# Scan over image rings: four strided history entries a ring, turned to rows one by one

## The reference

```python
# layer 0: relu, 3x3 depthwise convolution with dilation 2, 1x1 convolution, folded batch norm; x is (32, 56, 56, 256)
# layer 1: a scan over the pixels of the 56x56 image in spiral order, from the centre outwards
def step(g, inp):
    ci, ni, nm, nc = inp                       # this pixel, its four neighbours, their mask, their count
    local = g[:, ci, :]
    neigh = (g[:, ni, :] * nm[None, :, None]).sum(axis=1) / nc
    u = jnp.concatenate([local, neigh], axis=-1)
    y_sc = jnp.tanh(u @ w1 + b1) @ w2 + b2     # w1 is (512, 512), one scalar per image
    return g.at[:, ci, :].set(local + y_sc[:, None] * w_y[None, :]), None
```

## Time and profile before

| | |
|---|---|
| three runs, median | 4940.8 us (4936.70 to 4956.19) |
| the profiled execution, its span | 4956.47 us, 4954.6 us |
| busy share of the span | PE 91%, PEld 66%, DVE 81%, ACT 51%, POOL 70% |
| chain that ended last, by engine | PE 70%, ACT 10%, DVE 9%, issue 7%, DMA 2% |
| waits in the scan | PEld L868 for DVE L768: 197.5 us, 256 times; DVE L768 for ACT L554: 194.3 us, 344 times; PE L859 for DVE L704: 155.3 us, 293 times |

### The profile page before, as it was taken

One profiled execution on the slowest core, in us unless ns is written; L12 is line 12 of the kernel. 1 busy time (PEld: TensorE's weight loads), 2 busy tenths in 40 slices (PEclk: granted clock), 3 DMA queues, 4 the chain that ended last, 5 costly groups with the idle time before them and its releaser, 6 DMA issues.

```text
span 4954.6 us, 62164 instructions
## 1 busy us (share of the span) xinstructions
PE 4515.9 (91%) x19323; PEld 3290.4 (66%) x19323; DVE 4011.1 (81%) x6107; ACT 2520.8 (51%) x4454; POOL 3487.0 (70%) x2478
## 2 busy tenths in 40 slices
PE   3999999999999999999999999888888888888875
PEld 2788888888788888888878887644444444444432
DVE  5888888988886888888888887288888888877753
ACT  3566666666566566656656665333444443333321
POOL 3888888888887888888888888566666655554321
PEclk7999999999999999999999999999999999999976
DMA  3344444444444444444444443499999988876530
GB/s 92 116 130 139 132 138 134 135 137 134 132 137 135 132 139 131 138 129 140 131 137 132 139 127 126 168 310 298 294 317 288 285 273 259 242 226 188 166 107 27
DMA packets 395139, 835.31 MB, mean 169 GB/s; under 512 B 76864, under 2 KB 178496, under 8 KB 394688
## 3 DMA queue, kind: packets, MB, share of 16 engines
q1 hardware_dynamic: 251408, 420.08, 31.3%
q0 software_dynamic: 143408, 411.26, 22.2%
HBM read 419.95 MB, written 425.85 MB: 171 GB/s over the span
## 4 chain that ended last, share of the span: by engine, by line
PE 70%; ACT 10%; DVE 9%; issue 7%; DMA 2%; POOL 1%; SPq 0%; DVEq 0%; POOLq 0%; ACTq 0%
PE psum L846 12%; PE psum L848 12%; PE psum L847 12%; PE psum L830 12%; PE psum L859 10%; DVE psum L704 4%; ACT relu_rows L531 4%; PE psum L819 3%; PE psum L868 3%; PE psum L878 2%; PE psum L880 2%; DMA out<-dw_rows 2%; ACT u_hi L554 2%; PE psum L879 2%; ACT psum L549 2%
## 5 line engine op out<-in xcount | busy, mean ns | idle before, releaser
L629 DVE SCALAR_TENSOR_TENSOR dw_rows<-relu_rows,taps,dw_rows 128x1792 f32<-128x1792 f32 x872 | 1805.2, 2081 | 25.4 <-ACT dw_rows L520 20.3
L445 POOL DMA_INDIRECT s_x<-xo,wave_idx x784 | 1365.5, 1742 | 315.3 <-issue 215.9
L464 POOL DMA_INDIRECT out<-dw_rows x897 | 891.9, 994 | 860.4 <-DVE dw_rows L712 623.8
L846 PE MATMUL psum<-w_hi,u_hi 128*128 128x512 f32 x3136 | 1385.1, 442 | 0.0
L451 POOL DMA_INDIRECT s_pre<-eo,wave_idx x784 | 1207.8, 1541 | 247.5 <-issue 229.5
L848 PE MATMUL psum<-w_hi,u_lo 128*128 128x512 f32 x3136 | 1233.3, 393 | 0.0
L847 PE MATMUL psum<-w_lo,u_hi 128*128 128x512 f32 x3136 | 1226.4, 391 | 0.0
L859 PE MATMUL psum<-dw_rows,ident 128*128 128x512 f32 x1794 | 978.7, 628 | 161.5 <-DVE near L704 155.3
L485 ACT ACTIVATE eo<-psum 128x512 f32<-128x512 f32 x784 | 468.1, 597 | 1222.9 <-PE psum L848 1123.9
L549 ACT ACTIVATE psum<-psum 128x512 f32<-128x512 f32 x897 | 522.1, 582 | 914.2 <-PE psum L868 914.2
L830 PE MATMUL psum<-pw,dw_rows 128*128 128x256 f32 x3136 | 820.4, 385 | 63.7 <-ACT psum L540 59.4
(11 more groups left out here) (88 smaller groups left out, 3919.1 us busy)
## 6 DMA issues: line engine op xcount, KB each, us to landing
dw_rows<-s_pre SPq DMA_DIRECT2D x615, 256.0 KB, 3.9
x_tok<-x SPq DMA_DIRECT2D x112, 896.0 KB, 6.8
dw_rows<-s_x SPq DMA_DIRECT2D x615, 128.0 KB
dw_rows<-s_pre SPq DMA_DIRECT2D x169, 192.0 KB, 3.6
dw_rows<-s_x SPq DMA_DIRECT2D x169, 96.0 KB
out<-dw_rows POOLq DMA_INDIRECT x897
s_x<-xo,wave_idx POOLq DMA_INDIRECT x784, 3.3
s_pre<-eo,wave_idx POOLq DMA_INDIRECT x784, 3.4
```

The source lines that it names most:

```text
L445: pool.indirect_dma_start(s_x, bass.IndirectOffsetOnAxis(wave_idx[:, n:n + 1], 0), xo[:, n % XO_SLOTS, :], None, bounds_check=TILES * P - ...
L464: pool.indirect_dma_start(out_rows, bass.IndirectOffsetOnAxis(store_idx[:, c:c + 1], 0), o_t[:, c % OUT_SLOTS, :], None, bounds_check=OUT_ ...
L629: dve.scalar_tensor_tensor(out=dst, in0=pair_rows(relu_rows, k + ky - 1, c, 2 * kx * NB), scalar=taps[:, c, 3 * ky + kx:3 * ky + kx + 1], ...
L846: pe.matmul(bank, hi, w_hi[:, k, :], start=k == 0, stop=False)
```

## The change

The window of seven consecutive scalars becomes four with a step of two (positions 1, 3, 5 and 7 back, the only ones that carry a coefficient). They aren't reduced any more: each of the four products of a ring goes to a row of its own, so a group has four rows instead of one, and `sel` picks all four, so that the product in `add_sums` adds them. The second shifted product of `turn` is shifted by four columns instead of one. The three copies are written by the multiply itself.

The order changes too. On VectorE `neighbours` now stands directly behind the dot product, ahead of `finish`, and `sum_rows` stands last, at min(L + 2, use - 1).

```diff
-WIN = 7
+WIN = 4
...
-        sel[:, i] = ((part_i < 3 * B) & (part_i % B == i)) | (part_i == 3 * B) | (part_i == 3 * B + 1)
+        sel[:, i] = ((part_i < 3 * B) & (part_i % B // WIN == i)) | (part_i == 3 * B) | (part_i == 3 * B + 1)
...
-                dve.tensor_tensor(win[part][:, 0:n + 1, :], hist[:, g0:g1 + 1, level + 1:level + 1 + WIN],
-                                  coef_in_sb[:, at_in:at_in + (n + 1) * WIN].rearrange("p (g w) -> p g w", w=WIN),
-                                  ALU.mult).then_inc(win_ready, 1)
...
+                dve.tensor_tensor(terms(win[part], 0, n + 1, WIN),
+                                  thrice(hist[:, g0:g1 + 1, level + 1:level + 8:2], n + 1, WIN),
+                                  thrice(coef_in_sb[:, at_in:at_in + (n + 1) * WIN].rearrange(
+                                      "p (g w) -> p g w", w=WIN), n + 1, WIN), ALU.mult).then_inc(win_ready, 1)
+                win_ops += 1
...
-                dve.wait_ge(win_ready, S_COUNT[part, level])
-                dve.tensor_reduce(blocks(inner[part], 0, n + 1),
-                                  win[part][:, 0:n + 1, :].rearrange("p (o g) w -> p o g w", o=1).broadcast_to(
-                                      [P, 3, n + 1, WIN]), axis=AX.X, op=ALU.add).then_inc(in_ready, 1)
-                in_ops += 1
...
             for c in range(TILES):
                 dot(c)
+                for part, level in NEIGHBOURS_AT.get(c, ()):
+                    neighbours(part, level, c)
                 if c:
                     finish(c - 1)
                 for part, level in SUM_ROWS_AT.get(c, ()):
-                    sum_rows(part, level)
-                for part, level in NEIGHBOURS_AT.get(c, ()):
-                    neighbours(part, level, c)
-                for part, level in SUM_ROWS_NOW.get(c, ()):
                     sum_rows(part, level)
...
-                pe.matmul(t, b[:, 1:3 * B + 1], shift_sb[:, 1, :], start=False, stop=True).then_inc(s_turned, 1)
+                pe.matmul(t, b[:, WIN:3 * B + WIN], shift_sb[:, 1, :], start=False, stop=True).then_inc(s_turned, 1)
...
-        late = min(last + 1, use - 1)
         high.setdefault(min(last + 2, use - 1), []).append((part, level))
-        (rows_now if late == last else rows_late).setdefault(late, []).append((part, level))
+        rows.setdefault(min(last + 2, use - 1), []).append((part, level))
```

More of the change, by code:

```diff
@@ L179, in shape_tables @@
                 else:
-                    assert r2 == r - 1 and 1 <= d <= WIN and g2 - g == (q == 0)
-                    coef_in[rows, AT_IN[part, level] + (g2 - g0) * WIN + WIN - d] = 1.0 / len(near)
+                    assert r2 == r - 1 and d in (1, 3, 5, 7) and g2 - g == (q == 0)
+                    coef_in[rows, AT_IN[part, level] + (g2 - g0) * WIN + (7 - d) // 2] = 1.0 / len(near)
     part_i = np.arange(P)
@@ L280, in build @@
         wrap_sb = in_relu.take(2 * (LEVELS // 8)).rearrange("p (k n) -> p k n", k=2)
[L282 to L287, removed]
+        win_near = Region(near[:, :, :, :].rearrange("p a b c -> p (a b c)"), N_SLOTS * CK * NROW)
+        hist = win_near.take((GROUPS + 1) * HIST).rearrange("p (g n) -> p g n", g=GROUPS + 1)
+        shift_sb = win_near.take(2 * P).rearrange("p (k n) -> p k n", k=2)
+        own = [win_near.take(3 * B) for _ in range(2)]
+        win = [win_near.take(3 * B + WIN) for _ in range(2)]
         in_dw = Region(dw_rows[:, :, :, :].rearrange("p a b c -> p (a b c)"), D_SLOTS * CK * DROW)
@@ L343, in build @@
         win_ready = sem("win_ready")
-        in_ready = sem("in_ready")
         own_ready = sem("own_ready")
@@ L458, in _ @@
                 pool.memset(own[part], 0.0)
-                last = pool.memset(inner[part], 0.0)
+                last = pool.memset(win[part], 0.0)
             last.then_inc(cleared, 1)
@@ L714, in finish, with thrice, terms @@
                                          op1=ALU.add).then_inc(out_ready, 1)
[L716 to L722, removed]
+            own_ops, win_ops = 0, 0
+            def thrice(ap, n, w):
+                return ap.rearrange("p (o g) w -> p o g w", o=1).broadcast_to([P, 3, n, w])
+            def terms(buf, i, n, w):
+                blocks = buf[:, 0:3 * B].rearrange("p (k g w) -> p k g w", k=3, w=WIN)
+                return blocks[:, :, i:i + n, 0:w]
             def neighbours(part, level, c):
-                nonlocal own_ops, in_ops
+                nonlocal own_ops, win_ops
                 g0, g1 = groups_of(part, level + 1)
@@ L730, in neighbours @@
                 dve.wait_ge(y_ready, c + 1)
[L731 to L742 removed]
+                dve.tensor_tensor(terms(win[part], 0, n + 1, WIN),
[3 more added lines that the diff above has]
+                win_ops += 1
+                dve.tensor_tensor(terms(own[part], 0, n, 1),
+                                  thrice(hist[:, g0:g1, PAD + level:PAD + level + 1], n, 1),
+                                  thrice(coef_own_sb[:, at_own:at_own + n].rearrange("p (g w) -> p g w", w=1), n, 1),
+                                  ALU.mult).then_inc(own_ready, 1)
+                own_ops += 1
                 if level % 8 == WRAP_LEVEL:
@@ L746, in neighbours @@
                         body = level // 8
+                        s = g if q else g + 1
+                        dve.wait_ge(win_ready, win_ops)
+                        at = terms(win[part], s - g0, 1, 1)
+                        dve.scalar_tensor_tensor(out=at, in0=thrice(hist[:, s:s + 1, PAD:PAD + 1], 1, 1),
+                                                 scalar=wrap_sb[:, 1, body:body + 1], in1=at, op0=ALU.mult,
+                                                 op1=ALU.add).then_inc(win_ready, 1)
+                        win_ops += 1
                         dve.wait_ge(own_ready, own_ops)
[L748 to L751, removed]
+                        at = terms(own[part], g - g0, 1, 1)
+                        dve.scalar_tensor_tensor(out=at, in0=thrice(hist[:, g:g + 1, PAD:PAD + 1], 1, 1),
+                                                 scalar=wrap_sb[:, 0, body:body + 1], in1=at, op0=ALU.mult,
                                                  op1=ALU.add).then_inc(own_ready, 1)
                         own_ops += 1
[L754 to L762, removed]
+                assert (own_ops, win_ops) == SUMS_DONE[part, level]
             def sum_rows(part, level):
@@ L871, in turn @@
             def turn(part, level):
-                a, b = own[part], inner[part]
+                a, b = own[part], win[part]
                 t = psum[0:96, BANKS + part, 0:P]
-                own_n, in_n = SUMS_DONE[part, level]
+                own_n, wwin_n = SUMS_DONE[part, level]
                 pe.wait_ge(own_ready, own_n)
-                pe.wait_ge(in_ready, in_n)
+                pe.wait_ge(win_ready, wwin_n)
                 pe.matmul(t, a, ident[:, :], start=True, stop=False)
                 pe.matmul(t, b[:, 0:3 * B], shift_sb[:, 0, :], start=False, stop=False)
-                pe.matmul(t, b[:, 1:3 * B + 1], shift_sb[:, 1, :], start=False, stop=True).then_inc(s_turned, 1)
+                pe.matmul(t, b[:, WIN:3 * B + WIN], shift_sb[:, 1, :], start=False, stop=True).then_inc(s_turned, 1)
             pe.wait_ge(s_ready, 1)
@@ L898, in sums_order @@
 def sums_order():
-    neighbours, turns, high, rows_late, rows_now, count, done = {}, {}, {}, {}, {}, {}, {}
-    own_n = in_n = n = 0
+    neighbours, turns, high, rows, count, done = {}, {}, {}, {}, {}, {}
+    own_n = win_n = n = 0
     order = []
@@ L914, in sums_order @@
         count[part, level] = n
-        own_n, in_n = own_n + 1, in_n + 1
+        own_n, win_n = own_n + 1, win_n + 1
         if level % 8 == WRAP_LEVEL and part_of(level + 1, wrap_of(level)[0]) == part:
-            own_n, in_n = own_n + 1, in_n + 1
-        done[part, level] = own_n, in_n
+            own_n, win_n = own_n + 1, win_n + 1
+        done[part, level] = own_n, win_n
         neighbours.setdefault(last, []).append((part, level))
         turns.setdefault(min(last + 2, use - 1), []).append((part, level))
-        late = min(last + 1, use - 1)
         high.setdefault(min(last + 2, use - 1), []).append((part, level))
-        (rows_now if late == last else rows_late).setdefault(late, []).append((part, level))
-    return neighbours, turns, high, rows_late, rows_now, count, done
-NEIGHBOURS_AT, TURN_AT, HIGH_ROWS_AT, SUM_ROWS_AT, SUM_ROWS_NOW, S_COUNT, SUMS_DONE = sums_order()
+        rows.setdefault(min(last + 2, use - 1), []).append((part, level))
+    return neighbours, turns, high, rows, count, done
+NEIGHBOURS_AT, TURN_AT, HIGH_ROWS_AT, SUM_ROWS_AT, S_COUNT, SUMS_DONE = sums_order()
 NEAR_DONE = [sum(2 + (y < H - 1) + (y in (0, H - 1)) for y in (r % H for r in range(R + 1))) for R in range(ROWS)]
```

## The result

The changed kernel takes 5029.04 us (median of four runs, 5028.08 to 5035.85) beside 4946.43 us for the kernel before (four runs, 4936.70 to 4956.19): ratio 1.0169, 95% interval 1.0147 to 1.0190, so 1.7% slower, clear of the noise. The profiled execution took 5028.19 us, its span is 5026.4. One execution further down, of e5_quarter_x, took 7725 us at a mean granted clock of 0.62 and isn't compared.

What follows compares the result with a forecast made beforehand. No engine was taken as full in the later stages; what counts is which wait ends last. Stage terms -12 - 2 + 18 + 32 + 31 + 25 - 13 gave +79 us, 5020 us against the median, range 4985 to 5055.

Steps and rivals of the forecast that it cites:

- Four live groups: With four live groups, both parts' products wait for the rows' difference: 4.15 instead of 3.65 us per two tiles, +32 us.
- Three: With three live groups, two of three products wait: 7.22 instead of 6.24 us a level, +31 us.
- Five: With five live groups, part 0's product waits for the rows' difference: 8.97 instead of 8.39 us, +18 us.
- Two: With two live groups, the neighbours now stand in the chain: 3.07 instead of 2.68 us a tile, +25 us.
- Six: With six live groups, three tiles take 4.71 instead of 4.74 us, -2 us.
- Seven: With seven live groups, level 10.61 instead of 11.34 us, -23 us, taken as -12 because DMA's share would be 1.00.
- One: With one live group, the turn starts 0.44 instead of 0.86 us after the accumulator's read, -13 us if TensorE's clock stays.
- step of 1.18 us: With four live groups, TensorE needs 0.32 + 0.86 us from a product that waited to the next one.
- The later S that is free everywhere: Rival: the later rows' difference is off the path also at five to two live groups; 4914 us, chance 0.07.
- the lower clock with two live groups: Rival: with two live groups longer waits drop TensorE's clock, +29 us, 5049 us; chance 0.12.
- the higher one with one live group: Rival: with one live group the shorter level raises TensorE's clock, worth 42 us, 4978 us; chance 0.08.
- The place to stop at: On VectorE, the rows' difference starts 0.51 us after finish; by 0.40 the sum would be 25 us less.

Runs made afterwards that it cites:

- e5_quarter_x: The changed kernel, but SP loads only one ring of four of x_t per tile (result not the reference's); 5015.16 us, ratio 1.0136 to the kernel before.
- e3: The changed kernel with the rows' difference (sum_rows) directly behind the dot product, ahead of neighbours and finish, except with one live group; 4841.74 us, ratio 0.9772.
- e6: The changed kernel with eight result slots instead of four; 5009.77 us, ratio 1.0122 to the kernel before.
- e4: The changed kernel with the neighbours behind finish again, the rows' difference still last in its tile; 4999.07 us, ratio 1.0096 to the kernel before.
- e1: The changed kernel's data without a reduce, in the order of the kernel before; 4931.86 us, ratio 0.9954 to the kernel before.
- e8: The changed kernel with sum_rows directly behind the dot product, eight result slots and two extra TensorE products a tile in the last 30 tiles; 4795.30 us, ratio 0.9694.

## Why the prediction was right

The time was forecast at 5020 us, +79; it is 5029, +83, and by the right mechanism: S behind the neighbours and finish, in the chain of the waiting product. That the sum came so near is in part luck, since its terms miss in both directions: by the windows 9 us too little at four live groups and 6 at three, 7 too little gain at one. Step by step, forecast and measured in the windows:

- *Four live groups*, +32, measured +41. The term was too small. The pair takes 4.27 us and not 4.15. Of that, 0.10 is finish behind the dot product of the tile that waited: I used 0.68, and it is 0.78 (4301.10 to 4301.88). The other 0.02 to 0.04 lies in the neighbours: line 732 takes 0.26 us in this stage where it takes 0.20 in e3.
- *Three*, +31, measured +37, for the same 0.10 and the neighbours, which its one such pair of tiles passes.
- *Five*, +18, measured +19, but the pieces are not those of the forecast. From the product before it to the waited one it is 3.34 us (4014.15 to 4017.49) and not 2.82, since the product before it has its dot product after 1.45 and not 0.89; the four tiles from the waited product on (4008.46 to 4014.15) take 5.69 and not 3.20 + 2.95. The two errors of half a microsecond cancel: luck.
- *Two*, +25, measured +24.5. The 3.07 us a tile is there to the hundredth, and that too is two errors which cancel: behind S the read of the accumulator ends 0.86 after D (4750.31 to 4751.17, by the timeline) and not 0.82, and from there finish starts after 0.21 (4751.38) and not 0.25.
- *Six*, -2, measured -2.
- *Seven*, -12, measured -14. The bare level is 10.67, where 10.61 was forecast. But the step that halved the gain for the sake of DMA's full load was wrong in its reason: e6 runs at a higher load and reaches the bare level. The number held by luck: late stores took about as much (355.5 less 341.9, 13.6 us) as I had granted to the bytes (11).
- *One*, -13, measured -20. The turn comes 0.37 after the read and not 0.44, since TensorE starts 0.06 behind the last multiply, not 0.14 as behind the reduce. That makes -0.49 x 32 = -16, and the shortest level falls as much, from 4.42 to 3.94; the rest fits the granted clock, 0.66 instead of 0.63, but was not measured apart.

My step of 1.18 us from a waited product to the next was misread: in the earlier trace rows the chain enters that product late. It did no harm, since I added it to a dot product that I had counted as late by the same amount.

Of the rivals, the later S that is free everywhere is out by the wait at line 863, the lower clock with two live groups by 0.99 in the windows, and the higher one with one live group happened by three hundredths. The place to stop at, 0.51 from finish to S, measured 0.50 (4303.38, where finish starts by the timeline, to 4303.88), and e4 confirms what the rule in the Trainium skill ("VectorE: DVE Perf Modes", section "Two Vector instructions with no wait between them") says of it: S waits for the whole of whatever is ahead. The same rule would have given me the 0.10 that I missed: it counts the read of the accumulator as an instruction of its own, held when the last output into SBUF began in another group of partitions. S's does, and so behind S the read starts only when the dot product has ended, 0.78 after its start (4301.10 to 4301.88), and 0.68 after it elsewhere. The trace agrees: in the scan of the changed kernel the read starts 0.78 us after the dot product in all 412 cases behind S, and 0.67 to 0.68 in all 471 behind finish.

## What to carry to other kernels

In an engine's list, an instruction for which another engine waits belongs at the first place at which its own input is there. Earlier, it holds up what stands behind it (before and in e1, where S stood ahead of a dot product while the turn was still running: 234.5 us with four live groups). Later, each instruction placed ahead of it for tidiness is in the chain (here three of them: 275.6 instead of 220.9 in that stage, 187 us of 5029 in all). A move that frees a late instruction pays in the stage where it was on the path and costs in those where the thing moved behind it is: cut the profile by stage, and write the chain of one period for each. And a saved instruction is worth what it stood in: the data half of this change was worth 19 us in the old order and about 50 in the new one (5082 less 5029 by the medians, 1880.1 less 1830.2 by the scans).

## What the runs showed of the hardware that I had not expected

With one live group two products more for TensorE, without any use of their result, made the stage 27 us shorter, since the clock stayed at its upper level (0.96 instead of 0.66). A DMA share of 0.94 was no limit: the same traffic ran at 325 GB/s and a share of 0.97 when stores had eight slots, and at 328 and 0.98 in e8. The same small multiply took 0.26 us in the changed kernel at four live groups and 0.20 in e3; in the changed kernel an indirect store on GpSimd starts 0.03 us behind it (4303.15 and 4303.12), in e3 0.30 ahead of it (4250.30 and 4250.60). The changed kernel itself has both cases: with four live groups the store starts inside the multiply in 61 of 63, and these take 0.26 us; with five it starts 0.04 us ahead of it in 23, and these take 0.20. Whether that is the cause was not tried.
